# Convolution layer: the product tree and the residual term's sum on VectorE, one term summed by TensorE, norm statistics on ScalarE

## The reference, cut to what matters

```python
x = x + tanh(g_xattn) * conv_layer(layernorm(x), k, bias, ctx, ctx, 8)
x = x + tanh(g_ffn)   * moe(layernorm(x), router_w, gate_w, up_w, down_w)

def conv_layer(v, k, bias, x1, x2, num_heads):   # (8, 256, 512), 8 heads of a head group
    kv = v[:, :, :, None, :] * x2[:, :, None, :, :]       # outer product of the heads, 8 x 8
    y = causal_fft_convolution(kv, k)[..., :L]            # along L = 512
    y = y + kv * bias
    return einsum('bhijl,bhil->bhjl', y, x1)              # sum over the 8 heads i
```

## The kernel before, in words

| engine | order |
|---|---|
| TensorE | conv half 0 blocks 0 to 2; logits g-2; skip_turn g; block 3; sum_heads g-1; conv half 1; v_in g+2; x2_in g-1 |
| VectorE | product 00, 01; skip_sum; outer g+1 half 0; product 02; add_fours g-1; outer g+1 half 1; product 03; ln1 g+2; residual g-1; product 10; ln2 g-1; product 11, 12, 13 |
| GpSimd | add_pairs g-1; skip_last g-1; skip_first and kv_low g+1, half 0, then half 1 |
| ScalarE | xn2T_out g-2; kv_high g+1 half 0; logits_out; skip_out; kv_high half 1; root1, norm1 g+2; root2, norm2, xn2_out g-1 |

## Time and profile before

### The profile page before, as it was taken

One profiled execution on the slowest core, in us unless ns is written; L12 is line 12 of the kernel. 1 busy time (PEld: TensorE's weight loads), 2 busy tenths in 40 slices (PEclk: granted clock), 3 DMA queues, 4 the chain that ended last, 5 costly groups with the idle time before them and its releaser, 6 DMA issues.

```text
span 669.1 us, 11025 instructions
## 1 busy us (share of the span) xinstructions
PE 639.9 (96%) x3203; PEld 532.7 (80%) x3204; DVE 519.7 (78%) x655; ACT 240.5 (36%) x350; POOL 549.0 (82%) x354
## 2 busy tenths in 40 slices
PE   7998999999999999698998999999999999999995
PEld 7787888888887888588786878888888888888874
DVE  6878888888888888898899958699999948550601
ACT  5444443334443434245331332333333332333320
POOL 2999999999999999776186978789999878786852
PEclk9999999999999999899998999999999999999999
DMA  7445566666666564278677546367666644441110
GB/s 216 140 124 171 198 206 205 206 206 206 206 206 206 170 194 141 80 273 291 199 232 248 208 158 214 116 227 232 216 211 215 228 158 157 158 158 46 46 50 18
DMA packets 52642, 119.39 MB, mean 178 GB/s; under 512 B 5868, under 2 KB 6060, under 8 KB 52624
## 3 DMA queue, kind: packets, MB, share of 16 engines
q1 hardware_dynamic: 44464, 101.30, 46.6%
q0 software_dynamic: 4320, 12.72, 5.4%
q10 hardware_dynamic: 3840, 5.15, 2.8%
HBM read 94.08 MB, written 26.64 MB: 180 GB/s over the span
## 4 chain that ended last, share of the span: by engine, by line
PE 68%; DVE 19%; issue 6%; POOL 3%; ACT 1%; DMA 1%; DVEq 0%; ACTq 0%; POOLq 0%
PE pair L1508 25%; PE bank L1398 21%; PE bank L1524 13%; DVE kv L1128 3%; PE pair L1432 3%; DVE prod L1196 3%; PE bank L1539 2%; PE pair L1368 2%; POOL kv_lo L749 2%; DVE up L1302 1%; DVE prod L1164 1%; DVE gate L1302 1%; PE bank L1481 1%; DVE up L1305 1%; PE pair L1409 1%
## 5 line engine op out<-in xcount | busy, mean ns | idle before, releaser
L1398 PE MATMUL bank<-kv_hi,strip 128*128 128x512 f32 x640 | 211.7, 400 | 0.1
L749 POOL TENSOR_TENSOR kv_lo<-kv,kv_hi 128x2048 fp32r<-128x2048 f32 x30 | 138.6, 4618 | 4.8 <-DVE prod L1196 2.6
L1398 PEld LDWEIGHTS bank<-kv_hi,strip 128*128 128x128 f32 x640 | 121.1, 189 | 25.7 <-issue 1.1
L1398 PE MATMUL bank<-kv_lo,strip 128*128 128x512 f32 x320 | 125.3, 392 | 0.0
L1164 DVE TENSOR_TENSOR prod<-bank,cT 128x512 f32<-128x512 f32 x128 | 84.7, 683 | 20.9 <-PE bank L1398 20.9
L927 ACT ACTIVATE kv_hi<-kv 128x2048 fp32r<-128x2048 f32 x30 | 57.6, 1919 | 110.9 <-DVE kv L1128 87.2
L1508 PE MATMUL pair<-up,xT_hi 128*128 (+1 forms) x288 | 90.0, 394 | 3.6 <-DVE up L1305 3.0
L1508 PE MATMUL pair<-gate,xT_hi 128*128 x288 | 90.6, 396 | 0.9 <-DVE xT_lo L1322 0.6
L1398 PEld LDWEIGHTS bank<-kv_lo,strip 128*128 128x128 f32 x320 | 60.7, 190 | 11.4
L773 POOL TENSOR_TENSOR prod<-prod 128x2048 f32<-128x2048 f32 x14 | 64.5, 4606 | 5.0 <-DVE prod L1164 5.0
L1128 DVE TENSOR_TENSOR kv<-pair,cK 128x2048 f32<-128x2048 f32 x30 | 68.4, 2280 | 0.0
(11 more groups left out here) (195 smaller groups left out, 1171.7 us busy)
## 6 DMA issues: line engine op xcount, KB each, us to landing
raw<-gate_w SPq DMA_DIRECT2D x32, 512.0 KB, 3.8
raw<-down_w SPq DMA_DIRECT2D x32, 512.0 KB, 3.7
strip<-kparts SPq DMA_DIRECT2D x15, 1024.0 KB, 5.8
raw<-up_w SPq DMA_DIRECT2D x28, 512.0 KB, 4.4
sorted_x<-fill SPq DMA_DIRECT2D x12, 1056.0 KB, 5.4
xs<-sorted_x ACTq DMA_DIRECT2D x19, 256.5 KB, 2.7
x_in<-x_back SPq DMA_DIRECT2D x16, 256.0 KB, 5.5
cK<-ctx_back SPq DMA_DIRECT2D x16, 256.0 KB, 5.6
```

Of the source, the lines that this page charges most:

```text
L749: nc.gpsimd.tensor_tensor(kv_lo[u][:, hh, :], kv[:, hh, :], kv_hi[u][:, hh, :].bitcast(f32), ALU.subtract).then_inc(s_klo, 1)
L1398: last = nc.tensor.matmul(y_bank[lb][:, :], strip[u][:, 2 * hh + t, d * P:(d + 1) * P], v[u][:, hh, mb * COL:(mb + 1) * COL], start=(mb == ...
```

## The change

- GpSimd no longer adds pairs of terms, but for the first half of group 15. VectorE adds the terms of group g-1 in a tree at the head of stage g (`tree`: 2048, 1024, 512 elements), and adds the residual term J to it in a fourth step. `sum_heads` turns one term, with 4 transposes (group 15 keeps five terms).
- GpSimd's `skip_first` of g+1, half 0, waits for the whole tree of g-1; in stage 14 it waits for the choice of experts.
- ScalarE makes the sums of both norms by activations that also sum: minus the mean by Identity, the sum of squares by Square, then the root (`stats1`, `stats2`). VectorE keeps the reciprocal and the bias (`ln1_last`, `ln2_close`). Groups 0, 1 (norm 1) and 14, 15 (norm 2) stay as they were.
- The order on VectorE changes: `outer` of half 0 for g+2 stands at the end of stage g; `skip_sum` stands behind tree, two products and `ln1_last`. On TensorE conv half 0 is no longer split around `logits_of` and `skip_turn`, but in stage 14.
- `cK` is loaded one stage earlier. ScalarE casts the four chunks of the second gate matrix.

```diff
@@ SyncE, stage @@
-                    if known(g, lambda g: 0 < g < G - 1):
-                        load_cK(g + 1, 1 - u)
+                    if known(g, lambda g: g < G - 2):
+                        load_cK(g + 2, u)
@@ GpSimd @@
                 def skip_first(g, u, hh):
...
+                    if isinstance(g, int) and (g, hh) == (G - 1, 0):
+                        eng.wait_ge(s_hot, 1)
+                    elif hh == 0:
+                        wait(eng, s_tree, STEPS * (g - 1))
...
                 def stage(g, u, n):
-                    if isinstance(g, int) and g == 1:
-                        add_half_pairs(0, 0, 1)
-                    elif known(g, lambda g: g >= 2):
-                        add_pairs(g - 1, 1 - u)
@@ ScalarE @@
+                def stats1(g, u, n):
...
+                    nc.scalar.activation(xn[:, :], x_in[:, u, :], ACT.Identity, scale=-1.0 / L,
+                                         accum_out=nm1[:, 0:1]).then_inc(s_mean1, 1)
+                    act.wait_ge(s_mean1, g - 1)
+                    nc.scalar.activation(xn[:, :], x_in[:, u, :], ACT.Square, bias=nm1[:, 0:1],
+                                         accum_out=sq1[:, 0:1]).then_inc(s_square1, 1)
+                    act.wait_ge(s_square1, g - 1)
+                    nc.scalar.activation(sd1[:, :], sq1[:, :], ACT.Sqrt, bias=eps_t[:, 0:1], scale=1.0 / L)\
+                        .then_inc(s_sd1, 1)
...
+                    if choosing:
+                        logits_out(g - 2)
                     if more:
                         kv_high(g + 1, 1 - u, 0)
-                    if known(g, lambda g: g >= 2):
+                    if again:
+                        stats1(g + 2, u, n + 1)
+                        if not first:
+                            norm1(g + 2, u)
+                    if not choosing and known(g, lambda g: g >= 2):
                         logits_out(g - 2)
                     skip_out(g, u)
                     if more:
                         kv_high(g + 1, 1 - u, 1)
...
                     if before:
-                        root2(g - 1)
+                        if final:
+                            root2(g - 1)
+                        else:
+                            stats2(g - 1, 1 - u)
                         norm2(g - 1, 1 - u)
                         xn2_out(g - 1, 1 - u)
...
+                def gate_one_high_parts(chunks):
+
+                    for c in chunks:
+                        act.wait_ge(s_wraw[c], 48)
+                        nc.scalar.activation(slot_parts(GATE, 1, c)[0], raw[:, c, :], ACT.Copy).then_inc(s_whi, 1)
@@ VectorE @@
+                def tree(g, u):
+
+                    dve.wait_ge(s_p, (g + 1) * 2 * LB)
+                    nc.vector.tensor_tensor(prod[u][:, 0:4, :], prod[u][:, 0:4, :], prod[u][:, 4:8, :], ALU.add)\
+                        .then_inc(s_tree, 1)
+                    dve.wait_ge(s_tree, STEPS * g + 1)
                     nc.vector.tensor_tensor(prod[u][:, 0:2, :], prod[u][:, 0:2, :], prod[u][:, 2:4, :], ALU.add)\
-                        .then_inc(s_add2, 1)
+                        .then_inc(s_tree, 1)
+                    dve.wait_ge(s_tree, STEPS * g + 2)
+                    nc.vector.tensor_tensor(prod[u][:, 0, :], prod[u][:, 0, :], prod[u][:, 1, :], ALU.add)\
+                        .then_inc(s_tree, 1)
+                    dve.wait_ge(s_tree, STEPS * g + 3)
+                    dve.wait_ge(s_skp, g + 1)
+                    nc.vector.tensor_tensor(prod[u][:, 0, :], prod[u][:, 0, :], prod[u][:, J, :], ALU.add)\
+                        .then_inc(s_tree, 1)
@@ VectorE, stage @@
+                    if choosing:
+                        skip_sum(g, u)
+                    if before:
+                        tree(g - 1, 1 - u)
+                    if choosing:
+                        pick_experts(dve, 0, 0, G1)
                     product(g, u, n, 0, 0)
                     if first:
                         outer(1, 1, 0, 0)
                     product(g, u, n, 0, 1)
-                    skip_sum(g, u)
-                    if not first:
-                        outer(g + 1, 1 - u, n + u, 0)
+                    if again and not first:
+                        ln1_last(g + 2)
+                    if not choosing:
+                        skip_sum(g, u)
                     product(g, u, n, 0, 2)
-                    if known(g, lambda g: g >= 2):
-                        add_fours(g - 1, 1 - u)
                     outer(g + 1, 1 - u, n + u, 1)
                     product(g, u, n, 0, 3)
-                    if known(g, lambda g: g < G - 2):
-                        ln1(g + 2, u, n + 1)
-                    else:
-                        pick_experts(dve, 0, 0, G1)
...
                     if before:
                         residual(g - 1, 1 - u, n - 1 + u)
...
+                    product(g, u, n, 1, 0)
+                    product(g, u, n, 1, 1)
                     if before:
-                        ln2_first(g - 1, 1 - u)
-                        ln2_last(g - 1)
...
+                        ln2_close(g - 1)
                     product(g, u, n, 1, 2)
                     product(g, u, n, 1, 3)
+                    if again:
+                        outer(g + 2, u, n + 1, 0)
@@ TensorE @@
-                    terms = [0, 1, 2, 3, J] if five else [0, 1, J]
+                    terms = [0, 1, 2, 3, J] if five else [0]
...
+                    elif choosing:
+                        conv(g, u, n, 0, range(2))
                         logits_of(g - 2)
...
                         skip_turn(g, u)
+                        conv(g, u, n, 0, range(2, LB))
+                    else:
+                        conv(g, u, n, 0, range(LB))
+                        if known(g, lambda g: g >= 2):
+                            logits_of(g - 2)
                         skip_turn(g, u)
-                    if before and not second:
+                    if before:
                         sum_heads(g - 1, 1 - u)
```

More of the change, by code:

```diff
@@ L963, in stage @@
                         kv_high(g + 1, 1 - u, 1)
-                    if known(g, lambda g: g < G - 2):
-                        root1(g + 2)
+                    if first:
                         norm1(g + 2, u)
-                    if isinstance(g, int) and g == G - 1:
+                    if final:
                         act.wait_ge(s_y, (G - 1) * 2 * LB)
@@ L1106, in ln1, with ln1_last, ln2_close @@
                     dve.wait_ge(s_x[u], 16 * (n + 1))
-                    norm_first(x_in[:, u, :], mv1, ve1, s_var1, s_ln1, g)
-                    norm_last(mv1, sd1, rs1, nb1, s_sd1, s_xn, s_nb1, s_ln1, g)
+                    norm_first(x_in[:, u, :], mv1, ve1, s_var1, s_ln1, 3 * g)
+                    norm_last(mv1, sd1, rs1, nb1, s_sd1, s_xn, s_nb1, s_ln1, 3 * g, g)
+                def ln1_last(g):
+                    dve.wait_ge(s_sd1, g + 1)
+                    wait(dve, s_xn, g)
+                    nc.vector.reciprocal(rs1[:, :], sd1[:, :]).then_inc(s_ln1, 1)
+                    dve.wait_ge(s_ln1, g + 5)
+                    nc.vector.tensor_scalar(nb1[:, :], nm1[:, 0:1], rs1[:, 0:1], 1.0, ALU.mult, ALU.mult)\
+                        .then_inc(s_nb1, 1)
+                def ln2_close(g):
+                    dve.wait_ge(s_sd2, g + 1)
+                    wait(dve, s_xn2, g)
+                    nc.vector.reciprocal(rs2[:, :], sd2[:, :]).then_inc(s_ln2, 1)
+                    dve.wait_ge(s_ln2, g + 1)
+                    nc.vector.tensor_scalar(nb2[:, :], nm2[:, 0:1], rs2[:, 0:1], 1.0, ALU.mult, ALU.mult)\
+                        .then_inc(s_nb2, 1)
                 def k_low():
@@ L1209, in stage @@
                     first = isinstance(g, int) and g == 0
-                    second = isinstance(g, int) and g == 1
+                    choosing = isinstance(g, int) and g == G - 2
+                    again = known(g, lambda g: g < G - 2)
                     if final:
@@ L1433, in sum_heads @@
                                                     prod[u][:, i, lb * P:(lb + 1) * P], ident[:, :],
-                                                    start=(i == 0), stop=(i == J), is_transpose=True)
+                                                    start=(i == 0), stop=(i == terms[-1]), is_transpose=True)
                     last.then_inc(s_att, 1)
@@ L1443, in stage @@
                     before = known(g, lambda g: g >= 1)
-                    conv(g, u, n, 0, (0, 1, 2))
-                    if isinstance(g, int) and g == 0:
+                    first = isinstance(g, int) and g == 0
+                    choosing = isinstance(g, int) and g == G - 2
+                    if first:
+                        conv(g, u, n, 0, range(3))
                         v_in(1)
-                    if known(g, lambda g: g >= 2):
+                        conv(g, u, n, 0, range(3, LB))
+                        skip_turn(g, u)
+                    elif choosing:
+                        conv(g, u, n, 0, range(2))
```

(16 more changed lines are left out.)

100 lines of the change are left out of this document (60 added, 40 removed).

## The result

The changed kernel took 680.57 us (median of 4 runs, 678.6 to 681.15) against 670.72 (4 runs) for the kernel before beside it: ratio 1.0147, 95% interval 1.0125 to 1.017. It is slower, by 9.9 us; the forecast was 668.8 with 662 to 677. The profiled execution took 681.15 (span 679.4), so 10.3 more than the profiled one of before.

The account below looks back on a forecast made before the run. TensorE and GpSimd were taken as full together, 17.4 us a stage, and VectorE's waits as the bound after the conv. Terms +1.9 + 3.2 - 5.3 - 1.8 = -2.0 on 670.82 gave 668.8 us, range 662 to 677.

Parts of the forecast that it names:

- The clock: Rival: idle 1.5 us in each steady stage drops TensorE to its lower clock, 1.5 a stage: 687 us; chance 0.04.
- the step on the steady stage: Stages 2 to 13: a closed loop sets the period, 17.77 us against 17.61; 12 stages cost +1.9 us.
- The steady loop: Stages 2 to 13: VectorE's tree and skip_sum, then TensorE's turn and conv, close at 17.73 us, TensorE idle some 1.5.
- The statistics: ScalarE's two summing passes and root for x2: 2.0 us, between 1.5 and 2.6; their loop then gives 17.5.
- Both rivals: Late statistics on ScalarE: about 674 us, chance 0.13; square and root in different tables: about 698, chance 0.03.
- Entry: Groups 0 and 1: skip_turn at 40.3, TensorE idle 4.3 us, half clock added at half its price; +3.2 us (+2.4 to +4.0).
- Exit: Groups 14 and 15: choice of experts takes 1.5 us instead of 8, conv(15) at full clock; -5.3 us (-3 to -7).
- Behind the conv: After the conv: casts moved to ScalarE shrink TensorE's wait of 3.00 us; -1.8 us (-4 to +1).
- The lock: VectorE with two SBUF inputs and GpSimd reading SBUF exclude each other; each tree sum could wait up to 4.6 us.
- the forecast's own range: Whole kernel time from the bounds of the terms: 663.5 to 673.5 us.
- The 4.5 us taken from GpSimd buy nothing here: Steady stages: the tree is now in series with the outer products, the products and the turn, so no gain.

Follow-up runs that it names:

- the filler run: Changed kernel plus idle transposes of a constant on TensorE before skip_turn (14 a stage, 36 in stage 1): 670.41 us, ratio 0.999.
- four moves: Changed kernel with skip_sum ahead of the tree, ln1_last behind the residual, a product ahead of ln2_close, norm1 behind stats2: 663.57 us, ratio 0.9892.
- the half filler: Changed kernel plus half as many idle transposes on TensorE before skip_turn (7 a stage, 18 in stage 1): 675.45 us, ratio 1.0073.
- the two runs on the second `outer`: Kernel of the four moves, second outer of g+1 moved earlier on VectorE: ahead of all three products 697.96 us, behind two of them 668.7 us.
- three reordered kernels: Changed kernel with skip_sum ahead of the tree, 665.57 us; with four moves, 663.57; the latter with second outer one product earlier, 668.7.

## Why the prediction was wrong

**The step that failed is the rival "The clock"**, held at 0.04 "against: the granted clock is 1.00 in the steady stage, and in stage 14 the waits were about twice as long". The forecast's own sum has no term for the clock in the 12 stages. The 1.00 was read in a stage in which TensorE had 17.36 us of work in 17.40; the step on the steady stage had just put 1.5 us of idle time into each stage, so that row could no longer speak. Nor did "twice as long" help: waits of 1.3 to 1.66 were enough. Between the marks of group 1 and group 13 the clock fell to the lower level in 5 of 12 stages, 1.6 us each, and group 1's own stage lost 2.7, in all 10.6; the filler run gives back 10.2. The rival's price, 1.5 a stage, was right per fall; it didn't fall in every stage.

**The steady loop** was right: forecast 17.73, taken as 17.77, measured 17.82 in undisturbed stages. The tree 4.9, the two products, `skip_sum` behind them, TensorE idle 1.3 to 1.66 before `skip_turn`, GpSimd idle (5.2 before 168.67, where I had 4) are as written. 12 stages: +2.5 by the period (17.82 against 17.61) and +7.9 by the clock, where +1.9 stood.

**The statistics** took 1.9 us where I had 2.0 between 1.5 and 2.6, the first pass 0.61 and its reading instruction 0.19. `ln2_close` waits 1.40 for the root (about 1.5 forecast). No table is loaded inside the loop. Both rivals were rightly low.

**Entry**: forecast 40.3 for `skip_turn` with 4.3 idle, measured 40.30 with 4.09. The step after it, half a clock stretch at 0.8 us, was the miss: 2.7, hence +5.1 for +3.2. The row it came from was read short, and then halved: in stage 14 of the kernel before, the granted clock was 0.50 for 4.1 us of work (280.31 to about 284.4), not 3, and here it was 0.50 from 40.30 to about 46.

**Exit**: forecast -5.3, measured -5.2, the choice 1.5 us. The number is in part luck. The forecast had group 15's conv at full clock, but behind TensorE's wait of 1.98 (301.89) the granted clock was 0.50 from 302.5 to 305, and the last conv matmul came 38.6 behind group 13's instead of 37.6. The forecast's queue on VectorE left 1.2 us between that matmul and the last product, and this room took the fall in. The two runs on the wait for it show that it needs the tree's move: without the wait 3.1 us of the gain are lost before the last product and 8.0 in all by the medians; with the wait and GpSimd's pair sums still there it gives 1.0 at the last product and nothing that can be measured in the whole.

**Behind the conv**: forecast -1.8 (bounds -4 and +1), measured 0.0. The wait that was to shrink did go, and more: TensorE no longer stands 3.00 us before `up`, nor does its clock fall behind that wait (0.50 from 357 to 359 before). It began the next `down` 57.9 us after the last product (368.96) instead of 62.7 (363.47), so it was 4.8 ahead. One weight set later the lead was gone. VectorE, 3.6 ahead when the first `up` was split, lost nearly all of it: from there to the last `down_lo` its casts and low parts ran 11.7 us over their free times beside GpSimd, where it had been 8.4 (one took 3.27 at 388.48, for 1.23 when free). TensorE waited 4.2 us for `down_lo` in three waits, where it had waited 1.06 once. The first line is from the kernel before, the other two from the changed one:

```profile
386.59 0.50 PE L1524 MATMUL bank<-down_hi,hT_hi 128*128 128x512 f32 x1 [1.06 <-DVE down_lo L1305]
```
```profile
391.81 0.49 PE L1603 MATMUL bank<-down_hi,hT_hi 128*128 128x512 f32 x1 [2.25 <-DVE down_lo L1382]
```
```profile
388.48 3.27 DVE L1382 TENSOR_TENSOR down_lo<-raw,down_hi 128x1024 fp32r<-128x1024 f32 x1
```

With the casts back on VectorE the old waits came back, 2.97 before `up` and 1.02 for `down_lo`, at the same time in all. So the term failed because it priced the first wait of the chain alone; the next one, "a small one at 386", could only shrink in it, and it grew by 3.2.

**The lock** that I drew from the nearest rows was shown by the run without GpSimd's wait for the tree, 4.89 for 0.69. The Trainium skill, SBUF — State Buffer, Who interferes with whom, states the exclusive lock; that run agrees.

Taken together: without the falls of the clock up to group 13 the sum of the terms is +2.5 + 2.4 - 5.2 + 0.0 = -0.3, and the filler run measured -0.2 (670.41 against 670.58), inside the forecast's own range. That range itself was added up wrong: the bounds named for the terms give 664.1 and 674.7, not 663.5 and 673.5 (680.6 lies above either). "The 4.5 us taken from GpSimd buy nothing here" held too, but for a reason in the order, not in the idea: one instruction moved makes the change worth -0.8%, four moves -1.1%.

Open: why the clock falls in 5 of 12 stages. It fell behind a wait of 1.31 us (133.45) and not behind one of 1.66 (115.65), so the length of the single wait doesn't decide it alone. That a shorter wait keeps the clock is shown in the old place by the half filler (0.5 to 0.84 us, no fall in stages 2 to 13), and at a bank by the two runs on the second `outer` (waits of 1.04 us no fall, of 2.1 us a fall in 10 of 12 stages). Whether the place of the wait plays a part too is not shown.

## What to carry to other kernels

When your own sum puts idle time into an engine that had none, the clock of the old trace no longer holds: price the fall in that same step, stage by stage, as a likely case. Work taken off a full engine and put in series into another one's queue makes a loop; write the loop down and look which single move of a small instruction (here `skip_sum` ahead of the tree) cuts it. And before an instruction moves ahead of others, ask which bank each of these was about to free.

## What the runs showed of the hardware that I had not expected

Waits of 1.3 to 1.66 us, once in 17.8 us, are enough for TensorE to drop to 1.2 GHz again and again. Waits of 0.45 to 1.06 us, once in 17.3 to 17.8 us, weren't, in three reordered kernels and with the half filler. One fall costs 1.6 us in the middle stages of this conv, and 2.7 behind the wait of 4.09 in group 1's. Transposes of a constant were enough to hold the clock at 1.00 through the waits. A `TENSOR_SCALAR` on 128x8 with one input, 280.36 above, took 4.14 us beside GpSimd's pair sum (279.86, 4.60 long), where it took 0.17 in the run without the wait for the choice (297.99), so one small instruction is as exposed as a large one. A pass on ScalarE that also sums isn't dearer than a plain one (0.61 and 0.63; the Square, which also takes the mean as an operand, 0.72), but a reading instruction of 0.19 follows it, and the next pass starts 0.73 after the first.
